# Two layers with attention and experts: the schedule of the key products within the mLSTM heads, and of the token loads

## The reference

```python
ig = x @ Wi + bi;  fg = x @ Wf + bf              # gates, of q, k and v together
log_D = cumulated log_sigmoid(fg), causal, + ig
D = exp(log_D - max_log_D)                       # a row maximum, running over the keys
C = (qh @ kh.T / sqrt(32)) * D
h = (C / (max(|sum C|, exp(-max_log_D)) + eps)) @ vh
hn = (h - mean) * rsqrt(var + eps) * ln_scale
x = x + hn
...
k_img = rms_norm(ctx @ ki_w + ki_b)              # keys of the second attention
v_img = ctx @ vi_w + vi_b                        # its values
```

## Time and profile before

| what | us |
|---|---|
| median of the runs shown (3) | 1381.75 |
| their range | 1374.69 to 1386.12 |
| the profiled execution | 1377.97 |
| its span in the profile | 1376.3 |
| values stage, heads group 0, groups 1 to 3, tail | 196.1, 67.6, 180.9, 43.7 |

### The profile page before, as it was taken

How to read it: one execution, slowest core, us unless ns; L and a number is a source line. 1 busy time by engine, 2 the same in 40 slices (tenths; PEclk the granted TensorE clock), 3 DMA queues, 4 the chain that set the end, 5 groups by cost and what they waited for, 6 DMA issues and landing times. The chain is left out here.

```text
span 1376.3 us, 24515 instructions
## 1 busy us (share of the span) xinstructions
PE 1294.3 (94%) x7390; PEld 1071.6 (78%) x7391; DVE 830.6 (60%) x1598; ACT 748.7 (54%) x1848; POOL 389.6 (28%) x365
## 2 busy tenths in 40 slices
PE   7899976799999999999998989999989999999998
PEld 6688865577777768778886778888878888888887
DVE  3545545477766765354444467635477777777965
ACT  4334445587988542155446545544577555555551
POOL 0111024363828104469631054036001000000041
PEclk9999997899999899999999999999999999999999
DMA  8657895878687476475657887374565555555403
GB/s 290 235 214 254 298 301 191 283 216 282 210 273 245 161 215 261 154 242 175 206 145 248 288 262 233 98 247 148 192 190 159 166 159 168 159 163 155 125 33 123
DMA packets 168183, 280.99 MB, mean 204 GB/s; under 512 B 29920, under 2 KB 58336, under 8 KB 167840
## 3 DMA queue, kind: packets, MB, share of 16 engines
q1 hardware_dynamic: 142288, 224.44, 51.7%
q0 software_dynamic: 8672, 29.37, 6.5%
q10 hardware_dynamic: 17136, 26.09, 5.1%
HBM read 171.04 MB, written 108.80 MB: 203 GB/s over the span
## 5 line engine op out<-in xcount | busy, mean ns | idle before, releaser
L120 PE MATMUL banks<-of_shared_split,key_lead 128*128 128x512 f32 x256 | 108.8, 425 | 25.5 <-DVE key_trail L1405 21.5
L2986 ACT ACTIVATE prob<-banks,attend_row,rq 128x128 f32<-128x128 f32 x248 | 110.6, 470 | 0.0
L2999 ACT ACTIVATE attend_ol<-banks,of_attend_vbias 128x512 fp32r<-128x512 f32 x64 | 44.2, 691 | 116.3 <-PE banks L3198 116.3
L120 PE MATMUL banks<-wo,attend_ol 128*128 (+1 forms) x256 | 106.2, 415 | 0.0
L122 PE MATMUL banks<-of_shared_split,key_trail 128*128 128x512 f32 x256 | 103.7, 405 | 0.0
L121 PE MATMUL banks<-of_shared_split,key_lead 128*128 128x512 f32 x256 | 103.3, 403 | 0.0
L120 PE MATMUL banks<-queries_rows_split,queries_wl 128*128 128x512 f32 x256 | 100.9, 394 | 0.0
L122 PE MATMUL banks<-wo,attend_ot 128*128 (+1 forms) x256 | 100.7, 393 | 0.0
L121 PE MATMUL banks<-wo,attend_ol 128*128 (+1 forms) x256 | 99.9, 390 | 0.0
L122 PE MATMUL banks<-queries_rows_split,queries_wt 128*128 128x512 f32 x256 | 99.8, 390 | 0.0
L121 PE MATMUL banks<-queries_rows_split,queries_wl 128*128 128x512 f32 x256 | 99.7, 390 | 0.0
(11 more groups left out here) (399 smaller groups left out, 3558.4 us busy)
## 6 DMA issues: line engine op xcount, KB each, us to landing
mlstm_gmax<-running_max SPq DMA_DIRECT2D x36, 512.0 KB, 5.7
k_heads<-heads_key ACTq DMA_DIRECT2D x64, 256.0 KB, 4.5
q_heads<-queries_head SPq DMA_DIRECT2D x64, 256.0 KB, 2.9
q_ahead<-q_heads SPq DMA_DIRECT2D x64, 256.0 KB, 4.1
of_attend_k<-k_heads SPq DMA_DIRECT2D x60, 256.0 KB, 4.0
of_attend_v<-v_heads SPq DMA_DIRECT2D x60, 256.0 KB, 3.3
key_raw<-in_L_xattn_ki_w SPq DMA_DIRECT2D x20, 512.0 KB, 5.8
sorted_rows<-of_shared_split SPq DMA_DIRECT2D x2, 5120.0 KB, 28.7
```

The lines of the kernel that those rows point to most:

```text
L120: nc.tensor.matmul(out, lead_l, lead_r, start=first, stop=False)
L2986: ins = nc.scalar.activation(prob[:, j % 2, b, :], ps[:, j % 2, b * S:(b + 1) * S], ACT.Exp, bias=row[:, j % 2, 1, b:b + 1], scale=rq[:, b ...
L2999: nc.scalar.activation(ol[:, par, j, :], ps[:, 4 + j % 2, :], ACT.Identity, bias=vbias[:, bass.ds(quad_of(it) * 4 + j, 1)]).then_inc(ol_do ...
```

## The change

- Values stage: the four token loads leave the start of SP's queue and stand in its loop at `u` = 4, 5, 7 and 9 (the last three behind a wait for a finished unit). `STATS`, `NORMS` and the first gate come two units later, and the gates follow each other every 6 units (20, 26, 32, 38). At the end ScalarE makes two key weight leads and VectorE two trails.
- Heads: 12 key units in group 0, and `LAG` = 4 from then on, so four units are left after the last head. GpSimd's `early_lead` goes; ScalarE makes all leads.
- The copy of a turned quad moves from ScalarE to VectorE (behind `decayed`, ahead of the context sums and the trail).
- SP loads the context of the group after the next at heads 12 to 15 instead of 8 to 11; the split context of group 1 at heads 4 to 11 of group 0, that of later groups at once at head 10.
- Tail: the normalisation of the last group is placed anew between the four units.

```diff
-        STATS, NORMS = 6, 14
-        GATES = [18 + (UNITS - 13 - 18) // 3 * g for g in range(G)]
+        STATS, NORMS = 8, 16
+        GATES = [20 + (UNITS - 13 - 20) // 3 * g for g in range(G)]
+        TOKENS = {4: 0, 5: 1, 7: 2, 9: 3}
...
             load_ctx(2)
-            load_x(0)
             sp.wait_ge(turned, 2 * C)
             load_ctx(3)
-            for g in range(1, G):
-                load_x(g)
             sp.wait_ge(cleared, 1)
...
                     store_four(u // 4 - 1)
+                if u in TOKENS:
+                    if u > 4:
+                        sp.wait_ge(product, u - 1)
+                    load_x(TOKENS[u])
...
                         A.weight_lead(act, 0, 0)
+                        A.weight_lead(act, 1, 0)
...
             A.weight_trail(dve, 0, 0)
+            A.weight_trail(dve, 1, 1)
...
-    LAG = 8
-    OPENING = (0, 1, 2, 3, 6, 9, 12, 15)
+    LAG = 4
+    OPENING = (0, 1, 2, 3, 5, 6, 8, 9, 11, 12, 14, 15)
...
-                    if g + 2 < G and n == LAG:
+                    if g + 2 < G and n == PER - GB:
                         sp.wait_ge(ctx1_done, g + 2)
-                    if g + 2 < G and LAG <= n < LAG + GB:
-                        load_ctx(g + 2, n - LAG)
-                    if first and n >= LAG:
+                    if g + 2 < G and n >= PER - GB:
+                        load_ctx(g + 2, n - PER + GB)
+                    if first and LAG <= n < LAG + 2 * C:
                         A.load_split(sp, 1, n - LAG)
-                    if not first and not last and n >= PER - 2:
-                        if n == PER - 2:
-                            sp.wait_ge(product, CLOSES[g - 1] + 1)
-                        for part in range(C):
-                            A.load_split(sp, g + 1, (n - PER + 2) * C + part)
+                    if not first and not last and n == PER - 2 - LAG:
+                        sp.wait_ge(product, CLOSES[g - 1] + 1)
+                        for part in range(2 * C):
+                            A.load_split(sp, g + 1, part)
...
-                    if first and n + 1 in OPENING:
-                        early_lead(0, OPENING.index(n + 1))
...
-                if u == FIRST_OF[v] and v >= HALF:
-                    if v == HALF:
-                        act.wait_ge(wl_done, HALF)
+                if u == FIRST_OF[v] and v >= 2:
                     act.wait_ge(product, LAST_OF[v - 2] + 1)
...
-                    if n % 4 == 0:
-                        if n:
-                            quad(g, n // 4 - 1)
-                        elif not first:
-                            quad(g - 1, QUADS - 1)
-                    if not first or n == PER - 1:
-                        keys_at(g, n, 1, weight_lead, first)
+                    keys_at(g, n, 1, weight_lead, first)
...
+            def quad(g, c):
+                dve.wait_ge(quad_turned, g * QUADS + c + 1)
+                if c == 0 and g:
+                    dve.wait_ge(norm_done, FIRST + g - 1)
+                nc.vector.tensor_copy(hraw[:, half(g), :, 4 * c:4 * c + 4, :].rearrange("p b j e -> p b (j e)"),
+                                      ps[:, 0, :].rearrange("p (b w) -> p b w", b=GB)).then_inc(h_done, 1)
...
                     decayed(g, n + 1, first)
+                    if n % 4 == 0:
+                        if n:
+                            quad(g, n // 4 - 1)
+                        elif not first:
+                            quad(g - 1, QUADS - 1)
...
-            finish(PER - LAG)
+            quad(last, QUADS - 1)
             divisor(last)
             close(last, 0)
             close(last, 1)
-            for m in range(1, 4):
-                finish(PER - LAG + m)
+            finish(PER - LAG)
+            finish(PER - LAG + 1)
...
-            finish(PER - LAG + 4)
             variance(last, 0)
-            finish(PER - LAG + 5)
+            finish(PER - LAG + 2)
             variance(last, 1)
```

27 lines of the change are left out of this document (6 added, 21 removed).

## The result

The changed kernel takes 1366.14 us (median of 7 runs, 1361.49 to 1370.19) where the kernel before takes 1376.90 (7 runs, 1373.50 to 1386.12): a ratio of 0.9906, 95% interval 0.9882 to 0.9931. The gain is about 11 us, two fifths of the forecast 28, and under one per cent; the time lies 4 us above the forecast's own range. The profiled execution of the changed kernel took 1370.19 us, with a span of 1368.5.

What follows compares the result with a forecast made beforehand. TensorE was taken to lose time in group 0, waiting for key weights behind GpSimd's late leads and SP's held queue. Values -2.8, group 0 -10.6, groups 1 to 3 -5, tail -9.5: 1377.97 - 27.9, so 1350 us, range 1334 to 1362.

Steps and rivals of the forecast that it cites:

- The split loads are issued four heads before need: Groups 1 to 3: loads of the context halves keep their lead in heads, so nothing was booked for them.
- The other half of the step: Groups 1 to 3: quad copies on VectorE save 5 of the 8.7 us that TensorE waits for decayed scores.
- together 3.5 us for the three: Values stage: new waits at three gates spaced 6 units instead of 7, 3.5 us, bounds 0 and 5.7.
- The -4.6 and -2.3: Values stage: earlier value store removes TensorE's wait (booked -4.6 us) and the slow matmuls after it (-2.3 us).
- 3.3 + 4.3 + 1.8: Group 0 waits: unit 2's weight 3.3 us, trails behind quad copies at heads 4 and 8 4.3, turns without a unit 1.8.
- 2 us for slow matmuls: Group 0: slow matmuls after the wait for unit 2's weight, 2 us.
- over 0.9 was to show that the forecast is right: Group 0: sign of being right, TensorE's clock over 0.9 with 12 units in 53 to 61 us.
- One of its signs of being wrong: Group 0: masks still waiting over 10 us for loads; other signs were group 0 over 65 us, or new trail waits.
- The first rival: Group 0: transfers bound it, 16.9 MB taking 69 us, +1.4 instead of -10.6, kernel 1362 us; chance 0.13.
- The step with that wait: Tail: TensorE waits 3.6 us for a trail behind quad copy, divisor and row sums on VectorE.
- Two other terms: Tail: three units after the wait, 8.25 us; wait for the last sum of squares behind the normalisation, 2.8 us.
- VectorE's queue as a rival: At all 15 quads, copies hold up a trail until a unit is lost: 41 us against 28, 1391 us; chance 0.05.

Runs made afterwards that it cites:

- e1_split_first: Changed kernel with the eight split loads of context halves issued ahead of everything else of head 10 in SP's queue; 1359.6 us.
- e3_quad_act: Changed kernel with the quad copies back on ScalarE, ahead of the key weight's lead; groups 1 to 3 took 3.1 us more, group 0 lost 0.8 us.
- e18_eight_quad: Changed kernel with context halves first, eight units in group 0 and quad copies on ScalarE; group 0 59.0 us against 53.5 with the copies on VectorE.
- e2_gates7: Changed kernel with gates every 7 units from unit 18 again, later token loads kept; 1360.9 us, values stage 190.5 us.
- e9_pool_leads: Changed kernel with context halves first and leads of units 2 to 7 back on GpSimd; group 0 took 56.1 us.
- e12_all: e10_trail_first plus, in the tail, the first unit's trail ahead of the last group's divisor and row sums; tail 39.0 us instead of 35.3.
- e10_trail_first: Changed kernel with context halves first, gates every 7 units, and on VectorE the quad copy behind the next unit's trail; 1347.4 us.
- e11_ctx_only: Kernel before, with group 2's context loads at heads 12 to 15 of group 0 instead of 8 to 11; group 0 fell 2.5 us, kernel no faster.
- e13_second_weight: Kernel before, with both halves of unit 1's key weight made at the end of the values stage; group 0 fell by 4.8 us.

## Why the prediction was wrong

The span was to be 1348.4 us and is 1368.5. The 20.1 us are 10.4 in groups 1 to 3, 4.8 in the rest, 4.2 in the values stage, 1.1 in the tail, and 0.4 the other way in group 0.

**Groups 1 to 3, the step that failed:** "The split loads are issued four heads before need, as before, so I book nothing for them." The step counted heads and not microseconds, and took "as before" for "in time". In the kernel before TensorE already waited 3.8 us in two places for these halves, a row that the prediction did not read. In the changed kernel TensorE asked for them 7.9 us after the first was issued (303.46 less 295.53), with 9.3 us before (329.87 less 320.53), and the last landed some 12 us after the first was issued in both. The missing 1.4 us match the load of the turned context, 1.42 us of issue, which stands ahead of the halves at head 10 and not at head 14. So the waits grew to 6.6 us, and the clock fell behind them; e1_split_first prices this at 8.1 us. The second thing that the step left out is the clock: all new waits together only make up for those that went (13.2 us against 13.0), and the 5.3 us of busy time that the slow matmuls add are nearly the whole loss. The other half of the step was right: the waits for decayed scores fell by 5.7 us against the 5 booked, and e3_quad_act and e18_eight_quad show that the quad copies on VectorE are the reason.

**Values stage, the term that was mis-sized:** "together 3.5 us for the three, between 0 (the chain in front moves up with it) and 5.7." They cost 7.0 by e2_gates7. The forecast asked how much room a gate's chain has, and the spacing by itself costs 1.3 to 1.6 us. The other 5.4 came from a place that it never looked at: with the new numbers the store of the second gate falls on unit 30, where the first context half stores and all four context loads fall too. The -4.6 and -2.3 held in the changed kernel and in the four profiles with gates every 7 units. In five of the other seven with the values stage of the change the clock fell after the shorter wait too, so the -2.3 is not sure.

**Group 0** came out right in size (56.55 against 57), and that is in part luck. The forecast had 9.4 us of waits (3.3 + 4.3 + 1.8) and 2 us for slow matmuls. The trace has 4.4 us of waits (3.4 for trails, 0.8 for turned heads, 0.2 for a half), and TensorE is busy 52.2 us for the 43.4 us of booked work, at a clock of 0.88 where over 0.9 was to show that the forecast is right. One of its signs of being wrong came too: the masks still wait over 10 us for their loads, 27.6 us in all. So these waits alone do not set the time of the group. The prediction gave the blame to GpSimd's leads, late behind the masks, and SP's held queue. Alone, the queue was worth 2.5 us; unit 1's weight, made ahead of the group, 4.8; the leads and the quad copies about 5 each with eight units. With twelve units, undoing either costs 0.8 us at most (e9_pool_leads, e3_quad_act). The first rival, transfers as the bound, falls in its price: the 16.9 MB went at 299 GB/s and not at 247 (where they would take 68.4 us; the 69 of the prediction is a slip). As an idea it stands: the DMA share of the group is 0.93, against 0.70 before, and no run lightened the transfers alone. What limits a group of twelve units to 54 to 59 us in all these runs is not settled.

**Tail:** 35.3 against 34.2, with the wait of 4.01 where 3.6 stood. The step with that wait holds, and e12_all shows that another order on VectorE only moves it. Two other terms missed and nearly cancel: the three units after the wait took 11.2 us (447.02 to 458.25) where 8.25 was booked, and the wait for the last sum of squares was 0.68 us where 2.8 stood.

**VectorE's queue as a rival:** the price was small. The waits that the prediction named as agreeing with the rule were ScalarE's. The first-in, first-out order that the Trainium skill names (PSUM — Partial Sum Buffer, section Engine vs sequencer instructions) is seen here: TensorE waited for trails 3.3 us in five places in groups 1 to 3, up to 1.0 us each, where the kernel before had 0.5 us, and moving the trail ahead of the quad copy (e10_trail_first) halved such waits. The time of the groups did not follow.

Open: e11_ctx_only and e13_second_weight, whose code from group 1 on is that of the kernel before, took 187.0 and 187.2 us there instead of 180.9 and 180.6. So each lost again what it had won in group 0. Some 3.5 to 4 us of it are the clock: TensorE was busy 171.2 and 171.5 us there, and 167.7 and 167.4 in the two profiles of the kernel before. The rest is 2.6 to 2.8 us of further waits. Why the same code met them only in these runs is not known.

## What to carry to other kernels

When an edit moves a load nearer to its use, or a unit to another number, take the microseconds from issue to landing out of the trace and set them against the microseconds until TensorE asks; "as many heads ahead as before" is no margin where the kernel before already waited. List everything that the queue issues at each new number of the loop: a store that falls behind seven others is late for a reason that no dependency shows. Look at the busy time and the clock besides the waits: in groups 1 to 3 the waits were the same in sum and the stage was 5.4 us longer. And try parts alone before giving the credit: two parts that were worth 2.5 and 4.8 us in their own stage made the kernel no faster than the unchanged one, which gave a ratio of 0.9975 when it was measured again.

## What was not expected of the hardware

After waits of nearly the same length TensorE's granted clock can stay at full speed (2.4 GHz) or fall to half (1.2 GHz) for a while. After 2.94 us for a context half the kernel before ran on at full clock; after 2.75 us for the same load e11_ctx_only stood at a mean of 0.66 in the next 5 us, and its quad took 18.35 us where that of the kernel before took 17.02. The first long wait of the values stage tells the same, in kernels with the same code there: after 2.00 us e3_quad_act ran on at full clock, after 2.02 us e1_split_first had a mean of 0.66 in the next 5 us. The windows, in the order named:

```profile
332.81:337.80 4.99, 4.99 (x76) 3.97 (x76) 3.25 (x5) 3.20 (x8) 1.23 (x2) 1.00 0.80 302
```

```profile
329.86:334.86 5.00, 5.00 (x28) 3.59 (x32) 4.10 (x5) 1.64 (x3) 1.22 (x2) 0.66 0.88 328
```

```profile
51.99:56.99 5.00, 5.00 (x22) 4.12 (x23) 4.12 (x7) 1.20 (x2) 1.40 (x1) 1.00 1.05 404
```

```profile
53.19:58.19 5.00, 5.00 (x15) 3.95 (x16) 4.12 (x7) 0.98 (x2) 1.41 (x1) 0.66 1.05 399
```

So the price of a wait was not to be read from its length: it is the wait alone, or the wait and slow matmuls behind it. At the gate 3.25 us of wait cost some 5.4, and at the halves 6.6 us cost 8.1.
